# GpSimd's order at the end of the second attention pass: the powers of groups 30 and 31 ahead of the scatters of groups 26 and 27

## The reference

```
x = x + elu(attention(layernorm(x)))        # first attention pass, slope 0.2, one shared adjacency
x = x + mixture0(layernorm(x))              # 8 experts, the best 2 of each row, H = 256, gelu
x = x + relu(attention(layernorm(x)))       # second attention pass, slope 0.01
x = x + relu(expert1(layernorm(x)))         # 32 experts, the best 1 of each row, H = 32
```

## Time and profile before

| what | value |
|---|---|
| median of three timed runs | 1138.15 us |
| span of the profiled execution | 1195.3 us |
| time of the profiled execution | the page gives no other than its span |
| busy: TensorE, VectorE, ScalarE, GpSimd | 948.1, 791.0, 708.2, 781.6 us |
| second attention pass, last scatter issued | at about 917 us |
| last stage, first tile load issued | at about 927 us |

### The profile page before, as it was taken

How to read it: one execution, slowest core, us unless ns; L and a number is a source line. 1 busy time by engine, 2 the same in 40 slices (tenths; PEclk the granted TensorE clock), 3 DMA queues, 4 the chain that set the end, 5 groups by cost and what they waited for, 6 DMA issues and landing times. The chain is left out here.

```text
span 1195.3 us, 27365 instructions
## 1 busy us (share of the span) xinstructions
PE 948.1 (79%) x6789; PEld 839.2 (70%) x6789; DVE 791.0 (66%) x3492; ACT 708.2 (59%) x2414; POOL 781.6 (65%) x989
## 2 busy tenths in 40 slices
PE   5888988887179999999994899999960667666873
PEld 4677877776079999999994688888850555544653
DVE  6688898889459999999994378888873121121221
ACT  3998898886035656555552899999930333322431
POOL 4357777777617787877776048778785366666666
PEclk9999897987579999999997999999975655666555
DMA  9133432211367777777772113232213442223210
GB/s 207 37 120 118 139 102 61 60 51 38 95 180 207 203 205 206 208 203 207 196 203 60 36 51 87 76 86 76 60 42 109 109 111 83 74 82 85 64 35 8
DMA packets 147913, 130.88 MB, mean 109 GB/s; under 512 B 26450, under 2 KB 119484, under 8 KB 147760
## 3 DMA queue, kind: packets, MB, share of 16 engines
q1 hardware_dynamic: 125456, 93.02, 30.4%
q0 software_dynamic: 18272, 34.21, 8.4%
q10 hardware_dynamic: 4032, 1.89, 0.5%
HBM read 83.28 MB, written 49.61 MB: 111 GB/s over the span
## 5 line engine op out<-in xcount | busy, mean ns | idle before, releaser
L477 POOL DMA_INDIRECT xs<-staged,dst x256 | 258.9, 1011 | 77.6 <-issue 68.5
L1067 ACT ACTIVATE hT<-bank,wt 128x128 f32<-128x128 f32 x620 | 177.2, 369 | 133.4 <-PE bank L1274 81.4
L528 POOL DMA_INDIRECT out<-oq,xq x160 | 159.9, 999 | 112.2 <-DVE oq L978 66.3
L506 POOL DMA_INDIRECT x2d<-ob,xi x155 | 163.6, 1055 | 43.3 <-issue 29.1
L1260 PE MATMUL bank<-xnT,wt 128*128 128x128 f32 x1240 | 166.9, 278 | 0.7 <-issue 0.4
L1274 PE MATMUL bank<-w2s,hT 128*128 x1240 | 165.5, 276 | 0.7 <-DVE ob L951 0.5
L978 DVE SCALAR_TENSOR_TENSOR oq<-bank,xq 128x512 f32<-128x512 f32 x40 | 27.7, 692 | 197.1 <-remote 103.2
L1260 PEld LDWEIGHTS bank<-xnT,wt 128*128 128x128 f32 x1240 | 152.6, 194 | 3.1 <-issue 2.5
L1274 PEld LDWEIGHTS bank<-w2s,hT 128*128 128x128 f32 x1240 | 150.9, 192 | 1.8 <-issue 1.2
L1101 ACT ACTIVATE xnqT<-bank 128x512 f32<-128x512 f32 x40 | 23.9, 596 | 164.0 <-remote 71.0
L1016 ACT ACTIVATE p<-bank,nm 128x128 f32<-128x128 f32 x256 | 103.1, 403 | 19.1 <-DVE nm L699 13.9
(11 more groups left out here) (202 smaller groups left out, 2313.9 us busy)
## 6 DMA issues: line engine op xcount, KB each, us to landing
wt<-wpd SPq DMA_DIRECT2D x155, 258.0 KB
xq<-xs SPq DMA_DIRECT2D x160, 66.0 KB
xi<-xs SPq DMA_DIRECT2D x155, 66.0 KB
xb<-x2d SPq DMA_DIRECT2D x32, 258.0 KB
xb<-in_x SPq DMA_DIRECT2D x32, 256.0 KB
wpd<-w1c SPq DMA_DIRECT2D x56, 129.0 KB
xs<-staged,dst POOLq DMA_INDIRECT x256
out<-oq,xq POOLq DMA_INDIRECT x160
```

The lines of the kernel that those rows point to most:

```text
L477: pool.indirect_dma_start(out=xs[l], out_offset=bass.IndirectOffsetOnAxis(ap=dst[b % ND][:, c:c + 1], axis=0), in_=stag[s][:, q, 0:ROW], i ...
L506: pool.indirect_dma_start(out=x2d, out_offset=bass.IndirectOffsetOnAxis(ap=xi[t % NXI][:, ID:ID + 1].bitcast(U32), axis=0), in_=ob[:, t % ...
L528: pool.indirect_dma_start(out=orow, out_offset=bass.IndirectOffsetOnAxis(ap=xq[j % NXQ][:, q, ID:ID + 1].bitcast(U32), axis=0), in_=oq[j % ...
L1067: last = act.activation(hT[t % 2][:, j, :], HID[t % 2][:, j, :], ACT.Gelu, bias=wt[t % NW][:, c:c + 1])
```

## The change

In the second pass (l = 1) the loop makes the powers up to group 29 in the same places as before. The power of group 30 moves from step 35 to step 34, between the power of group 29 and the scatter of group 26, and that of group 31 from step 36 to step 35, between the scatters of groups 26 and 27. Nothing else is changed, and no instruction is added or taken away.

```diff
                 for i in range(max(leave) + 1):
-                    if (0, 5)[l] <= i < NG + 5:
+                    if (0, 5)[l] <= i < NG + 5 - 2 * l:
                         spreads(l, i)
+                    if l == 1 and NG + 2 <= i < NG + 4:
+                        spreads(l, i + 1)
                     if l == 0 and i == 3:
```

## The result

| what | before | after |
|---|---|---|
| median of the timed runs (4 each) | 1138.03 us | 1131.62 us |
| lowest to highest | 1137.34 to 1138.82 us | 1130.97 to 1132.99 us |
| span of the profiled execution | 1195.3 us | 1129.1 us |

The ratio is 0.9946 with a 95% interval of 0.9933 to 0.996: faster by 6.4 us. In three later sets of runs the changed kernel measured 0.9972, 1.0004 and 0.9987, so the first figure stands at the favourable end.

The account below looks back on a forecast made before the run. The prediction took the last scatter to set the last stage's start in timed runs (the fills in the profile). The fills' 4.6 us lead was hidden and scatters moved 0 us, so 1138.1 us, range 1135.5 to 1140.1.

Parts of the forecast that it names:

- Power 30 without a wait: GpSimd, second pass: group 30's power starts without waiting, 0.2 us to spare, its result at about 884.6 instead of 889.6.
- The rival in which GpSimd waits for the statistics of group 30: End of second pass: GpSimd idles before group 30's power, last scatter up to 1.9 us later, up to 1140.0; chance 0.20.
- Scatters of group 26 later at no cost: GpSimd, second pass: group 26's scatters start 1.5 us later, and nothing waits for one scatter alone.
- Power 31 earlier, no wait: GpSimd, second pass: group 31's power starts at 890.1 instead of 895.06, its statistics ready at 888.05.
- Lead of 4.6 us for the routing: VectorE, second pass: routing of group 31 begins at about 891.6 instead of 896.21, and `filli` comes at 897.8.
- Scatters stand: GpSimd, second pass: scatters of groups 27 to 31 keep their times, the last at 916.09 to 917.05; 0 us.
- The worth of the lead: Start of last stage: earlier fills gain 1.2 us in the profile, 0 in timed runs; bounds 0 and 4.6.
- The clock in the last stage: Last stage: a microsecond's shift against TensorE's 1.2 and 2.4 GHz stretches moves 2 to 3 us either way; chance 0.05.
- Is the slow pace there in a timed run?: SyncE's fills, second pass: probably issued every 0.52 us when timed, landing around 914, before the scatters' release at 919.5.
- The sum in the prediction: Profile's waits: 43.3 us in the last stage, 6.6 and 5.1 at the two passes' ends, 55.0 of 57 us excess.
- the stretched issue: SyncE and ScalarE issue slowly while GpSimd scatters; as a rival, real in timed runs too: gain 1.2 us, 1136.9; chance 0.22.
- The rival of the whole lead: Second pass: fills set their own pace, so all moves 4.6 us earlier, time 1133.6; chance 0.13.

Follow-up runs that it names:

- after again, first set: The changed kernel, unedited, run again beside the kernel before in the first later set: 1134.36 us, ratio 0.9972.
- e9: The changed kernel, unedited, run in the later set whose executions were all near 1195 us: 1195.25 us, ratio 1.0004.

## Why the prediction was wrong

**What holds now.** With the power of group 31 ahead of group 27's scatters, VectorE's routing and then the fills start about 4.5 us earlier against the scatters. The fills (32 x 128 rows) take far less of the DMA engines' time beside the last scatters (31.0% for 75.7%); in the traces the last scatter lands 2.27 us after its start and not 3.10, and the first load comes 0.8 us earlier. In three of the four traces with early fills and nothing else the clock then rises at about 6 us, so the first store is up to a further microsecond earlier and GpSimd pauses less at the start of the stage. From the last scatter's start to the last store's start it is 222.9 us on average in three traces of after and 226.4 in two of before: 3.5 us, beside 3.1 measured in the timed runs. That the place of the fills is the cause is shown: both kernels that put only it back lose the gain, and power 31 alone, which moves it, has the gain. That the clock carries most of it is argued, from two things. The kernel before with TensorE kept at work leaves the fills as they were and gains 4.4 us. And the one trace with early fills and a late clock (after again, first set) has the early load but takes 226.3 us in all, between the 225.5 and 227.4 of the kernel before. The changed kernel with TensorE kept at work doesn't decide it, as its clock fell back.

**By the steps of the prediction.**
1. Power 30 without a wait: right. 868.38 has no idle time before it. The rival in which GpSimd waits for the statistics of group 30 fell.
2. Scatters of group 26 later at no cost: right. The chain runs along GpSimd's own order and so through them, but the order is the same work in sum, and the last scatter is no later (step 5).
3. Power 31 earlier, no wait: right (875.61, no idle time before it).
4. Lead of 4.6 us for the routing: right. Against the last scatter `filli` is 4.5 us earlier (18.3 us ahead of it after; 13.8 in the kernel before traced again). The wait left is for TensorE, as said.
5. Scatters stand: right. From the start of the pass's first power to the last scatter's start it is 232.6 us after and 232.9 before (traced again).
6. **The worth of the lead, the step that failed.** "The lead of the fills is then hidden by the scatters" took it that scatters which start unmoved also land unmoved, and put the worth of the lead at 0 us; the timed runs gave 3.1. In the short kind the scatters do set the start; SyncE's queue waits for them 6.2 us in the kernel before and 10.1 after. But with fewer fills beside it the last scatter landed 0.8 us sooner, and the rest of the gain came behind it, in the stage that it starts (step 7). I had bounded the fills' lead from 0 to 4.6 as if only the fills' own end counted, and never asked what they cost the scatter that they run beside.
7. **The clock in the last stage**: "I can't work out; I give it 0.05 ... and 2 to 3 us". The size was about right, the chance far too low. The earlier trace rows showed 23 us of waiting ahead of the first store, and the trace's windows would have shown the stage entering at 1.2 GHz; a change to what happens just ahead of such a stage deserved a rival of its own.
8. **"Is the slow pace there in a timed run?"** The conclusion was right, the reading half right. Set beside the short trace of the same kernel (58.2 us less), the excess is 13.6 us up to the pass's first power (6.1 of it between the last scatter and the first load at the end of the first pass), 6.6 us between the last scatter and the first load of the last stage, nothing from there to the first store, and 38.1 us in the stores. The sum in the prediction had 5.1, 6.6 and 43.3: it came near the 57 in part by luck, as GpSimd waits for outputs in the short kind too and 7.5 us elsewhere were not in it. That the stretched issue makes those 38.1 us is not shown. And profiling doesn't make the excess: eleven of the fourteen traces taken later lack it, and in one set the timed runs have its length. So "the profile's span should come out at 1194.1" failed by 65 us; the trace after was of the other kind. In the long kind the 1.2 us came out about as put (1.1 against the same set's kernel before, 1.5 against the first trace).

The rule weighed there, in the Trainium skill (Runtime: NRT & Kernel Launch, the note on the profile's total against the reported time), of a fixed excess of about 6.2 us in the profiled total, shows in no execution here: the span is 1.9 us under the same execution's time. Neither the 57 us nor the trace after goes by it.

The rival of the whole lead, 4.6 us and 1133.6, comes nearest to the pooled mean of 1134.7, and by another mechanism. The rest of the first result, 1131.62, is not reproduced: the changed kernel's later medians are 1134.36 and 1135.78.

**What stays open.** Why the clock rises earlier after an early start, when one trace with early fills still took 29 us, isn't settled. A stage that starts 1 to 2 us earlier could fall otherwise against whatever decides the clock, and that would make the gain a matter of phase; no run shifted the start alone. Power 30 alone leaves the fills where they were and still measured 1.6 us under before; of that there is no account, but it is hardly more than the 1.4 us between two runs of one kernel in the same set. What makes an execution of the long kind is unknown. A kernel with the fills left out altogether, which would give the landing of a lone scatter, wasn't tried.

No version clearly beats the changed kernel. The kernel before with TensorE kept at work is level with it or a little ahead (1133.53 ± 0.88 against 1134.72 ± 0.48), and the two together, as far as the clock held, are no better.

## What to carry to other kernels

When a transfer is off the critical path, ask what it runs beside: moving 32 small fills away from the last scatters let these land 0.8 us sooner, though neither the fills nor the scatters' issue was late. Where a stage opens with TensorE at 1.2 GHz after a pause, what shifts its start by a microsecond may move the time by three, and keeping TensorE at work through the pause is worth a trial by itself (0.4% here); look in the trace whether the clock held. And where a trace is longer than the timed runs by several per cent, take another trace before explaining the excess: its critical chain may not be that of the runs.

## What the runs showed of the hardware that I had not expected

- Executions of one program come as 1138 us or 1195 us. All timed executions of a set were of one kind; the first trace of before is of the long kind beside short timed runs. In the long, sixteen of SyncE's fills in the second pass start within 19.0 to 23.5 us while GpSimd scatters, in the short within 8.5 beside the same scatters. In the long kind GpSimd waited 111.8 us ahead of its stores, 66.8 of it for outputs, against 63.3 and 15.5 in the short; groups by line, changed kernel, GpSimd 915 to 1195 us, the long kind (e9) and then the short (trace after):

```profile
L530 POOL DMA_INDIRECT out<-oq,xq x160 | 160.3, 1002 | 111.8 <-DVE oq L980 66.8 <-issue 45.0
```
```profile
L530 POOL DMA_INDIRECT out<-oq,xq x160 | 157.4, 984 | 63.3 <-issue 47.9 <-DVE oq L980 15.5
```

- The last scatter's landing grew from 2.27 us to 3.10, 3.71 and 4.72 us as the fills' lead over it shrank from 16.9 us to 12.4, 12.5 and 10.4. At leads of 12.4 and 12.5 it took 3.10 to 3.71 us in five traces, so other things enter. At 15.6 and more it took 2.27 in all five.
- From the start of work in the last stage to 2.4 GHz it took from 6 to 34 us, with the same instructions. In the changed kernel with TensorE kept at work the clock was at 2.4 GHz when the stage began and fell to 1.2 from 2.8 to 9.6 us behind its first VectorE instruction, with TensorE at work from 908.1 us on.
